# Deformable and ternary convolutions on one core: weight folds moved into GpSimd's loop, low parts shared out anew, transposes mixed with the last offset convolutions

## What is computed

```python
x = x + L0(gn(x))      # gn: group norm, 32 groups
x = x + L1(gn(x))
# L0: deformable convolution, then group norm in 16 groups, gamma and beta
om = conv3x3(x, w_off) + b_off            # 27 maps: 9 dy, 9 dx, 9 mask
mask = sigmoid(m)
sampled = bilinear(x, py, px) * mask      # 9 taps, zero outside the image
out = einsum("bckhw,ock->bohw", sampled, weight) + bias
# L1: two convolutions with weights in -1, 0, 1, batch norms and relu
q = ternary_quantize(w)                   # thresholds from mean, max and min of all of w
out1 = relu(bn(conv3x3(x, q1)));  out = relu(out1 + bn(conv3x3(out1, q2)))
```

## Time and profile before

| | us |
|---|---|
| three runs | 294.27, 295.69, 296.38 |
| their median | 295.69 |
| the profiled execution | 296.87 |
| its span, from first to last instruction | 295.1 |
| busy in the span: PE, DVE, ACT, POOL | 256.5, 195.5, 170.8, 136.5 |

### The profile page before, as it was taken

How to read it: one execution, slowest core, us unless ns; L and a number is a source line. 1 busy time by engine, 2 the same in 40 slices (tenths; PEclk the granted TensorE clock), 3 DMA queues, 4 the chain that set the end, 5 groups by cost and what they waited for, 6 DMA issues and landing times.

```text
span 295.1 us, 5557 instructions
## 1 busy us (share of the span) xinstructions
PE 256.5 (87%) x1980; PEld 221.3 (75%) x1980; DVE 195.5 (66%) x450; ACT 170.8 (58%) x365; POOL 136.5 (46%) x193
## 2 busy tenths in 40 slices
PE   1878997999989999998999989999899949999900
PEld 1646765889978899897998889988677737777700
DVE  5697616679987999579978699781465343105094
ACT  2565756689777978877898787860043024330051
POOL 9085457477857778886678966240000000000040
PEclk9995996699999999999999999999999986999965
DMA  7905367634443332333323343100000000000006
GB/s 237 344 27 170 120 220 238 207 114 141 136 130 107 124 99 71 113 109 119 104 78 95 114 134 112 48 0 2 0 0 2 0 0 0 0 3 0 4 36 253
DMA packets 25737, 28.13 MB, mean 95 GB/s; under 512 B 2525, under 2 KB 23629, under 8 KB 25704
## 3 DMA queue, kind: packets, MB, share of 16 engines
q1 hardware_dynamic: 25200, 26.47, 27.3%
q10 hardware_dynamic: 504, 1.24, 1.3%
HBM read 19.87 MB, written 6.78 MB: 90 GB/s over the span
## 4 chain that ended last, share of the span: by engine, by line
PE 70%; DVE 18%; ACT 7%; issue 2%; DMA 2%; SPq 0%
PE PS L776 24%; PE PS L699 6%; PE PS L585 5%; PE PS L652 5%; PE PS L681 5%; PE PS L683 5%; PE PS L700 5%; PE PS L701 5%; PE PS L682 5%; DVE slo L1286 4%; ACT vhi L947 2%; DVE st L1186 2%; DVE vlo L1297 2%; DVE xb L1389 2%; DMA xs<-in_x 2%
## 5 line engine op out<-in xcount | busy, mean ns | idle before, releaser
L498 POOL TENSOR_TENSOR vt<-rowm,hat 128x1026 f32<-128x1026 f32 x36 | 70.7, 1965 | 35.9 <-PE PS L661 35.0
L1297 DVE TENSOR_TENSOR vlo<-PS,vhi 128x576 fp32r<-128x576 f32 (+2 forms) x88 | 50.0, 589 | 17.4 <-ACT vhi L947 16.9
L947 ACT ACTIVATE vhi<-PS 128x576 fp32r<-128x576 f32 (+2 forms) x88 | 43.8, 523 | 20.5 <-PE PS L683 20.3
L1286 DVE TENSOR_TENSOR slo<-PS,shi 114x512 fp32r<-114x512 f32 (+1 forms) x68 | 43.2, 675 | 6.8 <-ACT shi L935 6.4
L681 PE MATMUL PS<-shi,patch 114*128 114x288 f32 (+1 forms) x136 | 44.2, 325 | 1.6 <-DVE omr L1441 1.1
L699 PE MATMUL PS<-vhi,wdhi 128*128 128x256 f32 x144 | 43.7, 304 | 1.8 <-ACT xb L954 1.8
L518 POOL TENSOR_TENSOR xb<-xb,xs 128x512 f32<-128x512 f32 x3 | 3.7, 1278 | 87.0 <-ACT xb L1019 87.0
L776 PE MATMUL PS<-xhi,q 128*128 128x512 f32 (+1 forms) x144 | 39.1, 419 | 4.2 <-ACT xhi L1014 4.2
L683 PE MATMUL PS<-shi,patch 114*128 114x288 f32 (+1 forms) x136 | 41.4, 304 | 0.0
L682 PE MATMUL PS<-slo,patch 114*128 114x288 f32 (+1 forms) x136 | 41.2, 303 | 0.0
L700 PE MATMUL PS<-vlo,wdhi 128*128 128x256 f32 x144 | 40.5, 281 | 0.0
(11 more groups left out here) (155 smaller groups left out, 436.4 us busy)
## 6 DMA issues: line engine op xcount, KB each, us to landing
patch<-xt SPq DMA_DIRECT2D x136, 114.0 KB
xt<-xtt SPq DMA_DIRECT2D x4, 1024.0 KB, 6.1
xs<-in_x SPq DMA_DIRECT2D x3, 512.0 KB, 7.6
out<-xb SPq DMA_DIRECT2D x6, 256.0 KB, 2.3
wraw<-in_L_conv_w SPq DMA_DIRECT2D x2, 576.0 KB, 9.3
wd_raw<-in_L_conv_weight ACTq DMA_DIRECT2D x1, 576.0 KB, 7.0
xs<-in_x SPq DMA_DIRECT2D x2, 256.0 KB, 4.6
omr<-omr SPq DMA_DIRECT2D x8, 64.0 KB, 3.8
```

The source lines that it names most:

```text
L498: g.tensor_tensor(vt[:, n % 2, :, :].rearrange("p t (r j) -> p t r j", r=WR), rowm[:, n % 2, :, :].unsqueeze(3).to_broadcast([P, TAPS, WR, ...
L947: last = a.activation(places(vhi), src, ACT.Copy)
L1286: d.tensor_tensor(lo, src, hi, ALU.subtract).then_inc(slo_ok, 1 if pairs(n) == 2 else 3)
L1297: last = d.tensor_tensor(places(vlo), src, places(vhi), ALU.subtract)
```

## The change

It moves work and removes none; what is computed stays the same.

- POOL: the eight folds leave the place ahead of the loop. All four of w1 run at n = -4, behind `distances(1)` and ahead of `outer(0)`; those of w2 run one in each of n = 0 to 3. POOL makes the low parts of images 0 and 2, DVE those of 1 and 3.
- PE: `turn_image(1)` goes ahead of `offset_conv(1, 1)`; `offset_conv(3, 1)` goes behind `turn_offsets(2)`, between slots -2 and -1; in slot 0 `turn_pairs_out(2)` and `turn_last_out(2)` go ahead of `sample(0, 1)`, right behind `turn_offsets(3)`.
- ACT: the transfer of `wd_raw` is issued behind the first table load; `tail(2)` and `pixels_hi(1)` go ahead of `heads(GN0, 2)`, `hats(1)` ahead of `masks(1)`.
- DVE: the statistics of image 2 go ahead of `scale_shift(GN0, 1)`; the low part of image 0 is gone, that of image 1 stands behind `deviation(GN0, 2)`; `scale_shift(GN0, 2)` stands behind the offsets of image 0; `pixels_lo(1)` and `pixels_lo(3)` go each one step up.
- SP: the copies of `replicate(2)` and `replicate(3)` are issued behind the windows of chunks 4 and 5.

```diff
@@ -404,10 +404,10 @@
             fetch_patches(2)
             store_pixels(3)
             fetch_patches(3)
-            replicate(2)
-            replicate(3)
             for n in range(PATCHES, CHUNKS):
                 fetch_patches(n)
+                if n - PATCHES in (0, 1):
+                    replicate(2 + n - PATCHES)
             for n in range(CHUNKS - PATCHES, CHUNKS):
                 sp.wait_ge(patch_in[n % PATCHES], patches_through(n))
 
@@ -453,20 +453,24 @@
             g.iota(colw[:, :], [[1, W]], base=0, channel_multiplier=0).then_inc(consts, 1)
             g.iota(byi[:, :], [[TR, NT], [1, K], [0, K], [1, TR]], base=-1, channel_multiplier=0).then_inc(consts, 1)
 
-
-            pool.wait_ge(gn_ok, 2)
-            for i, arrived in enumerate((w1_in, w2_in)):
-                pool.wait_ge(arrived, 16)
-                n = C * TAPS
-                for level in range(FOLDS):
-                    src = wraw[i] if level == 0 else fold[i]
-                    n //= 2
-                    g.tensor_tensor(fold[i][:, 0:n], src[:, 0:n], src[:, n:2 * n], ALU.add).then_inc(tern_fold, 1)
-                    pool.wait_ge(tern_fold, FOLDS * i + level + 1)
-
-                pool.wait_ge(*((xn_ok, 2) if i == 0 else (xn_late, 1)))
-                pool.wait_ge(xhi_ok, i + 2)
-                g.tensor_tensor(inner(xlo, 1 + i), square(plain(1 + i)), inner(xhi, 1 + i), ALU.subtract).then_inc(xlo_pool, 1)
+            def fold_weights(i, level):
+
+                n = C * TAPS >> level + 1
+                if level == 0:
+                    pool.wait_ge((w1_in, w2_in)[i], 16)
+                else:
+                    pool.wait_ge(tern_fold, FOLDS * i + level)
+                src = fold[i] if level else wraw[i]
+                g.tensor_tensor(fold[i][:, 0:n], src[:, 0:n], src[:, n:2 * n], ALU.add).then_inc(tern_fold, 1)
+
+            def low_parts(b):
+
+                pool.wait_ge(xn_ok, 1) if b == 0 else pool.wait_ge(xn_late, b - 1)
+                pool.wait_ge(xhi_ok, b + 1)
+                g.tensor_tensor(inner(xlo, b), square(plain(b)), inner(xhi, b), ALU.subtract).then_inc(xlo_pool, 1)
+
+            low_parts(0)
+            low_parts(2)
 
             def distances(n):
 
@@ -510,6 +514,11 @@
                     outer(n + 3)
                 if n + 5 < CHUNKS:
                     distances(n + 5)
+                if n == -4:
+                    for level in range(FOLDS):
+                        fold_weights(0, level)
+                if 0 <= n < FOLDS:
+                    fold_weights(1, n)
                 if n >= CH and n % CH in (7, 8):
                     add_y(n // CH - 1, n % CH - 7)
 
@@ -569,10 +578,10 @@
                     pe.wait_ge(xhi_top, 1)
                 elif not part:
                     pe.wait_ge(xhi_ok, b + 1)
-                elif b in (1, 2):
-                    pe.wait_ge(xlo_pool, b)
+                elif b in (0, 2):
+                    pe.wait_ge(xlo_pool, b // 2 + 1)
                 else:
-                    pe.wait_ge(xlo_ok, 1 + b // 3)
+                    pe.wait_ge(xlo_ok, b // 2 + 1)
                 if (b, h) == (1, 0):
                     pe.wait_ge(wd_ok, 1)
                 if (b, h) == (1, 1):
@@ -629,15 +638,14 @@
             offset_part(1, 0, 0)
             turn_offsets(0)
             offset_part(1, 0, 1)
+            turn_image(1)
             offset_conv(1, 1)
-            turn_image(1)
             turn_image(2)
             offset_conv(2, 0)
             turn_offsets(1)
             turn_image(3)
             offset_conv(2, 1)
             offset_conv(3, 0)
-            offset_conv(3, 1)
 
             def turn_pairs_out(n):
 
@@ -751,20 +759,23 @@
                 if n >= 0:
                     sample(n, 0)
                 if n == 0:
+
                     turn_offsets(B - 1)
+                    turn_pairs_out(n + 2)
+                    turn_last_out(n + 2)
                 if piece_at(n, 0):
                     combine(*piece_at(n, 0))
                 if n >= 0:
                     sample(n, 1)
                 used = None
-                if n >= 0 and n + 1 < CHUNKS:
+                if n > 0 and n + 1 < CHUNKS:
                     pe.wait_ge(slo_ok, 3 * n + 6)
                     used = beside(n)
-                if n + 2 < CHUNKS:
+                if n and n + 2 < CHUNKS:
                     turn_pairs_out(n + 2)
                 if piece_at(n, 1):
                     combine(*piece_at(n, 1))
-                if n + 2 < CHUNKS:
+                if n and n + 2 < CHUNKS:
                     if used:
                         pe.wait_ge(*used)
                     turn_last_out(n + 2)
@@ -798,6 +809,7 @@
 
             slot(-2)
             turn_offsets(2)
+            offset_conv(3, 1)
             slot(-1)
             for n in range(SPECULATED):
                 slot(n)
@@ -859,10 +871,10 @@
         def _(act):
             a = nc.scalar
             act.dma_start(woff_raw[:, :], w_off.rearrange(flat)).then_inc(woff_in, 16)
-            act.dma_start(wd_raw[:, :], wd.rearrange(flat)).then_inc(wd_in, 16)
             act.wait_ge(zeroed, 2)
             act.dma_start(boffc[GRP:GRP + OFFC, :], b_off.rearrange("(c a) -> c a", a=1)).then_inc(boff_in, 16)
             a.activation(warm[:, :], warm[:, :], ACT.Sqrt)
+            act.dma_start(wd_raw[:, :], wd.rearrange(flat)).then_inc(wd_in, 16)
             act.wait_ge(zeroed, 4)
             act.wait_ge(woff_t, 1)
             a.activation(woff_part(0), woff_sum, ACT.Copy).then_inc(woff_hi, 1)
@@ -1041,16 +1053,16 @@
             root(GN0, 2)
             a.activation(warm[:, :], warm[:, :], ACT.Sigmoid)
             masks(0)
+            tail(2)
+            pixels_hi(1)
             heads(GN0, 2)
-            tail(2)
             tail(3)
-            pixels_hi(1)
             heads(GN0, 3)
             pixels_hi(2)
             hats(0)
             tail(4)
+            hats(1)
             masks(1)
-            hats(1)
             pixels_hi(3)
             tail(5)
             tail(6)
@@ -1423,13 +1435,14 @@
             image_stats(GN0, 1)
             deformable_lo(0)
             deviation(GN0, 1)
-            tails(GN0, 0)
+            dve.wait_ge(x_in[2], 16)
+            image_stats(GN0, 2, last=False)
             scale_shift(GN0, 1)
-            for b in (2, 3):
-                dve.wait_ge(x_in[b], 16)
-                image_stats(GN0, b, last=b == B - 1)
+            dve.wait_ge(x_in[3], 16)
+            image_stats(GN0, 3)
             deformable_lo(1)
             deviation(GN0, 2)
+            tails(GN0, 1)
 
             def pixels_lo(b):
                 dve.wait_ge(xthi_ok, b + 1)
@@ -1444,19 +1457,19 @@
             dve.wait_ge(pads, 11)
             deformable_lo(2)
             pixels_lo(0)
-            scale_shift(GN0, 2)
             offsets(0)
             offsets(1)
+            scale_shift(GN0, 2)
             whole_late(2)
+            pixels_lo(1)
             whole_late(3)
             largest(0)
-            pixels_lo(1)
             tails(GN0, 3)
             pixels_lo(2)
             offsets(2)
             offsets(3)
+            pixels_lo(3)
             largest(1)
-            pixels_lo(3)
             slot(-2)
             offsets(4)
             offsets(5)
```

## The result

| | before | after |
|---|---|---|
| median (runs), us | 295.69 (4) | 291.54 (4: 290.55, 290.57, 292.52, 292.67) |
| ratio, with 95% interval | | 0.9876 [0.9837, 0.9915] |
| a second comparison, median (runs) | 296.36 (11) | 291.16 (6) |
| its ratio | | 0.9821 [0.9776, 0.9866] |
| profiled execution, span | 296.87, 295.1 | 290.57, 288.8 |

The changed kernel is 1.2 to 1.8% faster. Over all the runs of this study (44 later runs of the kernel before, 10 of the changed one) the medians are 296.1 and 291.2, 4.9 us apart; the two profiled executions lie 6.3 us apart.

A forecast was written before the change was run, and what follows sets the result against it. The prediction took PE to bound the loop, so prologue savings reach the end. Its terms, -1.3 - 2.5 + 0.7 - 2.7 = -5.8 us, took the median from 295.69 to 289.9 us, range 286.8 to 293.5.

The forecast's parts named there:

- signs that the prediction named for being right: Profile marks: short L1138 and L1139, L1137 about 1.5 us, PEclk 1.00 from 20 to 37 us, slot 3 near 56, others.
- three that it named for being wrong: PEclk at 0.50 in slots 0 to 2, PE waiting for `vt` at slot -2, or wd landing past 10 us.
- What bounds the kernel: In the loop from 57 us on, PE is the bound, so what the prologue saves arrives at the end.
- The transfer of wd: Prologue: issued at about 3.4 us, image 0 comes 1.0 us earlier, PE's turns start at 9.0; PE gains 0.1 us.
- The hold of L1137: Prologue, DVE: POOL's low part of image 0 holds L1137 until 15.0 instead of 13.64; PE's `group_square(1)` starts 1.3 us late.
- The first rival: Prologue: L1137 gets in ahead of POOL, 1.3 us more is gained, 288.6 us; chance 0.22.
- Pair 2: Prologue, PE: `group_square` of pair 2 comes at 21.4 instead of 22.74 us, gain 1.3 us, bounds 0.3 and 2.6.
- The first low stretch: PE, 22.7 to 29.9 us: the half clock, which followed a 2.51 us wait, stays up; gain 2.5 us (0 to 2.5).
- The folds ahead of `outer(0)`: POOL before slot -2: w1's folds cost 3.2 us but are covered with 0.9 us to spare, so nothing is lost.
- The fourth rival: POOL's folds in front of `outer(0)` make `vt` late for PE, slower than before, 299 us; chance 0.04.
- Slots -2 to 2: PE, start of the loop: a gain of 2.7 us, about the middle of the bounds 0 and 5.6.
- The second rival: The clock falls again in slots -2 to 2, only 0.3 of the 2.7 us is left, 292.3 us; chance 0.2.

The follow-up runs named there:

- a0: The changed kernel itself, run and profiled again as reference for a later series: 291.16 us, ratio 0.9821 against the kernel before.
- e4: The changed kernel with PE's turns of chunk 2 in slot 0 put back behind the second sample: 291.20 us, ratio 0.9839 against the kernel before.
- e6: The changed kernel with w1's folds also taken from ahead of `outer(0)`, all eight run in n = 0 to 3: 290.71 us, ratio 0.9841.
- e3: The kernel before with only the folds moved into the loop as in the changed kernel: 292.03 us against 296.36, ratio 0.9860.
- e1: The changed kernel with the transfer of `wd_raw` issued early again, where it was before: 290.52 us, ratio 0.9805 against the kernel before.
- e5: The changed kernel with `offset_conv(3, 1)` put back ahead of slot -2: 292.05 us, ratio 0.9880 against the kernel before.
- e8: The changed kernel with image 0's low part on DVE, `wd_raw` on SyncE's queue and seven extra unread matmuls on PE: 291.30 us, ratio 0.9864.

## Why the prediction was right, and where it was not

The forecast was 289.9 us, the range 286.8 to 293.5; measured were 291.54 and, in the second series, 291.16 against 296.36. Of the signs that the prediction named for being right, all are in the profile (L1137 at 1.13 us where some 1.5 was named). Of the three that it named for being wrong, all came too, in part: the clock reads 0.50 for 3.4 us in slots 0 and 1, `wd_raw` landed at 10.1 us, and PE stood 0.1 us for `vt` at slot -2. So the path is the one that was forecast, and three of its terms were not what they were said to be. By the steps:

**What bounds the kernel.** Right. From slot 3 to the second ternary convolution (its first matmul on PE behind the batch norm) it takes 181.61 us before and 181.77 after; nearly all that was gained at slot 3 (5.87 us) arrived there (5.71). That matmul in the kernel before and in the changed one:

```profile
243.54 4.13 PE L776 MATMUL PS<-xhi,q 128*128 128x512 f32 x9 [4.21 <-ACT xhi L1014]
...
237.83 3.67 PE L787 MATMUL PS<-xhi,q 128*128 128x512 f32 x9 [4.21 <-ACT xhi L1026]
```

**The transfer of wd.** Here the working failed. ACT's queue issued it while the table load was still running, and not at 3.4:

```profile
1.77 1.28 ACT L876 ACT_TABLE_LOAD   x1 [1.77 <-DVE eps L1142]
1.84 0.36 ACTq L877 DMA_DIRECT2D wd_raw<-in_L_conv_weight  x1
```

It landed 8.3 us later, not 5.6. The turns began at 10.21 (8.88 in a0, 9.06 to 9.20 in e4 to e6) against 9.0 forecast. Image 0 came 1.1 us earlier, as said, but e3, with the early issue, has its second half earlier still, and e1, with the early issue too, at 6.89: how much of it the move makes is not shown. In time the move cannot be told from nothing (e1).

**The hold of L1137.** Right in place, direction and size: ended at 15.06 where 15.0 was worked out, and held in every profile with GpSimd's low part of image 0 and the late `wd_raw` (1.13, 2.09, 1.96, 1.90 and 1.57 us). The first rival needed it ahead of POOL; that came only with the early transfer (e1). The Trainium skill, SBUF — State Buffer, "Who interferes with whom", says that issue order decides who blocks. The traces agree both ways, with about 0.1 us between the two starts: DVE at 13.92 and POOL at 13.97 in e1 (0.22 us for DVE), DVE at 12.86 and POOL at 12.75 in a0 (2.09 us). DVE's own low part of image 3 is held in the same way: it starts at 28.86, behind POOL's of image 2, and takes 2.25 us instead of 1.22, which the prediction has not; no wait of PE shows from it.

**Pair 2.** 21.4 forecast, 21.12 measured. But in a0 it was 22.42, and here is the term that was mis-sized: the clock of the first matmuls. I counted the low stretches that PEclk shows and not the one from the start of the program, where PEclk reads 1.00 and only the pace of the matmuls tells (0.43 us against 0.25), with the moment at which the trace's record of the clock begins. That is 12.8 us in the profile of before, 13.2 in that of after, 18.3 in a0. Of the 1.3 us of gain, 0.3 are left in such an execution. That was the lower bound I gave, for another reason.

**The first low stretch.** Gone, as forecast, in all the profiles but e3's; twelve matmuls and 24 turns at full pace. Two and a half us were counted, and about 2.6 are there. The reason given for it was not right, or not whole: the prediction tied the fall to the wait of 2.51 us ahead of it, but in e3 that wait is 0.40 us and the clock falls all the same, 0.9 us behind the 24 turns. What kept it up in the changed kernel, whose order behind pair 2 differs as well, no run separates; that the term came out is in part luck. From pair 2 to slot -2 it took 20.41 us before and, with `offset_conv(3, 1)` added back, 16.86 + 2.27 = 19.13 after: 1.3 net, where 2.5 - 0.7 = 1.8 was forecast. The waits are what differs: 0.94 us for the low part of image 2, since DVE's `whole_late(3)` came in ahead of POOL (between the 0.5 taken and the 1.3 of the bound), and up to 0.2 for `vt`.

**The folds ahead of `outer(0)`.** 0.9 us of cover forecast, none left: POOL waited 0.93 us for the shifted copies of the offsets, which I had not put into its list though the profile of before has 0.67 us of it, and ended `vt` at 37.92. It cost 0.2 us (e6). The fourth rival lives on this chain and was never near.

**Slots -2 to 2.** 2.7 us forecast, 2.85 measured between the end of `offset_conv(3, 0)` and slot 3 (21.05 before, 18.20 after). The mean between the bounds was a guess that held; e4 and e5 divide it, 0.76 and 1.15 us with the rest only in both. The second rival (the clock falls again) came true in part: in the changed kernel it fell in slot 0 for 3.4 us and not 10.2 (6.8 in e5, not at all in e6 and e8), and cost 0.3 to 0.6 us: from slot -2 to slot 3 it takes 17.56 and 17.62 us in e6 and e8, 17.88 to 18.12 in the eight profiles with 3.4 us of it.

**The time.** At slot 3 the forecast was 56 us, the profile says 56.06, and the span is 288.8 against 289.3. The median moved by less, 4.15 us in four runs and 5.2 in the larger series. The profile of before (296.87) was from the upper part of its kernel's runs, that of after (290.57) from the lower part of its own, which reaches to 292.67; 4.9 us between all runs is 0.9 less than the 5.8 of the sum, and executions like the profiled one of a0 (292.14), 1.3 us later at pair 2 and 1.1 at slot 3, are of the size to explain it. How often they come is not known, so that they do explain it is likely, not shown.

## What to carry to other kernels

Look for tiny VectorE instructions whose duration is that of a GpSimd instruction beside them: here two of them, of two elements a lane, cost about 4 of 296 us (2.7 to 5.6 by the interval of e3), through PE's wait and a longer stretch at the lower clock, and moving GpSimd's work by 13 us or more gave 4.3 of the 5.2 us of the change. Moving other GpSimd work into the same chain takes some back, so put GpSimd's long instructions where DVE handles PSUM (in the profile after, a low part of DVE with one input in PSUM takes 0.76 us at 49.31, inside POOL's `vt` from 49.16 to 51.13), and check each for what DVE does in those two microseconds. When transposes and matmuls both have to be done, try to alternate them: with two such moves slots -2 to 2 took 3.0 us less here.

## What the runs showed of the hardware that was not expected

- A DMA issue in ACT's queue is not held by a table load: issue at 1.84 us, load from 1.77 to 3.05.
- A transfer of 576 KB issued in the first two microseconds landed after 5.1 to 8.3 us (5.7, 6.0 and 7.0 in three kernels with the early issue on ACT's queue; 7.0 to 8.3 in six profiles with the late one; 5.1 to 6.1 in five profiles on SyncE's, ahead of images 1 to 3). The changed kernel alone gave 8.3 and 7.0.
- PE's clock rose for the first time at 9.2 to 18.3 us, with PE's first work at 3.9 to 4.7 us in all kernels, and the changed kernel's two profiles differ by 5 us in it (13.2 and 18.3).
- A float32 matmul of 128 x 128 ran as two instructions of about 0.25 us at the lower clock, a float32 transpose of that size as one of 0.24.
